# A block with a selective scan, attention and routed experts on one core: scores computed twice, probabilities never turned

## The reference, cut to what matters

```python
x = x + tanh(g_xattn) * ssm_forward(ctx_1024, layernorm(x), ...)
# in the second part, per batch element:
q, k = rope(h @ wq + bq, h @ wk + bk);  v = h @ wv + bv
scores = einsum('bqhd,bkhd->bhqk', q, k) * HEAD_DIM ** -0.5
scores = where(causal, scores, finfo.min)
attn = softmax(scores, axis=-1)
ctx = einsum('bhqk,bkhd->bqhd', attn, v);  x = x + ctx @ wo
# scan, per step t:
state = state * exp(d_t * A) + (d_t * u_t) * B_t;  y_t = state . C_t
```

## Time and profile before

| | |
|---|---|
| median of 3 runs | 1940.85 us (1940.26 to 1944.68) |
| profiled execution, its own time | 1938.13 us |
| its span, first to last instruction | 1936.3 us |
| busy: PE, PEld | 1546.4 us (80%), 1184.4 us (61%) |
| busy: DVE, ACT, POOL | 1221.5 us (63%), 888.3 us (46%), 786.2 us (41%) |
| mean granted clock of TensorE, of full | 0.853 |

### The profile page before, as it was taken

One profiled execution on the slowest core, in us unless ns is written; L12 is line 12 of the kernel. 1 busy time (PEld: TensorE's weight loads), 2 busy tenths in 40 slices (PEclk: granted clock), 3 DMA queues, 4 the chain that ended last, 5 costly groups with the idle time before them and its releaser, 6 DMA issues.

```text
span 1936.3 us, 26458 instructions
## 1 busy us (share of the span) xinstructions
PE 1546.4 (80%) x9104; PEld 1184.4 (61%) x9104; DVE 1221.5 (63%) x1730; ACT 888.3 (46%) x1973; POOL 786.2 (41%) x744
## 2 busy tenths in 40 slices
PE   5346877777957778767769676899999999999994
PEld 2234544455635555544547444778878899999973
DVE  4789669987488986599873452433232566656545
ACT  3433446664356662566642564121121466666510
POOL 0595145542255441355432021144321455555544
PEclk8555977888967788968889687999999999999997
DMA  5620001110101110001101111812120477777464
GB/s 192 235 77 22 23 11 33 55 45 27 40 22 50 53 36 28 11 28 55 45 23 66 55 34 50 347 63 101 60 71 1 183 251 263 244 252 258 156 234 157
DMA packets 92372, 191.54 MB, mean 99 GB/s; under 512 B 8704, under 2 KB 25600, under 8 KB 88912
## 3 DMA queue, kind: packets, MB, share of 16 engines
q1 hardware_dynamic: 87120, 173.07, 26.0%
q0 software_dynamic: 5120, 16.78, 2.6%
HBM read 136.21 MB, written 53.61 MB: 98 GB/s over the span
## 4 chain that ended last, share of the span: by engine, by line
PE 40%; DVE 6%; issue 5%; ACT 3%; POOL 3%; DMA 0%; DVEq 0%; ACTq 0%; SPq 0%; POOLq 0%
PE scores L526 21%; PE bank L526 12%; DVE HS L1370 2%; POOL yab L1924 2%; PE scores L645 1%; DVE YA L1380 1%; PE bank L673 1%; PE bank L658 1%; PE bank L823 1%; PE bank L590 1%; ACT EX L1035 1%; ACT PT L1043 1%; ACT bank L1000 1%; DVE nm L1422 1%; POOL lal L1917 1%
## 5 line engine op out<-in xcount | busy, mean ns | idle before, releaser
L1781 POOL TENSOR_TENSOR GB<-DU,BB 128x512 f32<-128x512 f32 x256 | 327.4, 1292 | 138.8 <-DVE HS L1370 83.4
L590 PE MATMUL bank<-ident,HS 128*128 128x128 f32 x896 | 190.8, 351 | 181.0 <-DVE YA L1380 126.4
L1370 DVE TENSOR_TENSOR_SCAN HS<-bank,GB 128x512 f32<-128x512 f32 x224 | 270.4, 1207 | 33.7 <-ACT bank L1000 15.5
L590 PEld LDWEIGHTS bank<-ident,HS 128*128 128x128 f32 x896 | 128.7, 176 | 231.8 <-DVE YA L1380 167.2
L1000 ACT ACTIVATE bank<-DL,aneg 128x512 f32<-128x512 f32 x224 | 155.0, 692 | 139.3 <-DVE HS L1370 138.0
L1380 DVE SCALAR_TENSOR_TENSOR YA<-bank,Ct,YA 128x512 f32<-128x512 f32 x224 | 164.8, 736 | 27.5 <-PE bank L590 25.2
L526 PE MATMUL scores<-xth,wgh 128*128 128x256 f32 x552 | 158.0, 286 | 2.0 <-DVE fa L1667 1.1
L1043 ACT ACTIVATE PT<-bank 128x128 f32<-128x128 f32 (+3 forms) x256 | 110.3, 431 | 107.2 <-PE bank L658 106.2
L526 PE MATMUL scores<-xth,wgl 128*128 128x256 f32 x552 | 156.1, 283 | 0.0
L526 PE MATMUL scores<-xtl,wgh 128*128 128x256 f32 x552 | 156.0, 283 | 0.0
L658 PE MATMUL bank<-ident,EX 128*128 128x128 f32 x640 | 132.5, 316 | 26.5 <-ACT PT L1043 24.9
(11 more groups left out here) (241 smaller groups left out, 3816.4 us busy)
## 6 DMA issues: line engine op xcount, KB each, us to landing
wgr<-wffn_in SPq DMA_DIRECT2D x108, 384.0 KB, 6.5
wdr<-wffn_in SPq DMA_DIRECT2D x81, 256.0 KB, 3.2
BB<-b_scratch SPq DMA_DIRECT2D x64, 256.0 KB, 3.2
xg<-V SPq DMA_DIRECT2D x1, 11776.0 KB, 39.2
xr<-xg SPq DMA_DIRECT2D x23, 512.0 KB, 5.7
yg<-ysb SPq DMA_DIRECT2D x23, 512.0 KB, 6.4
hah<-hhd SPq DMA_DIRECT2D x5, 1024.0 KB, 6.0
hal<-hhd SPq DMA_DIRECT2D x5, 1024.0 KB, 8.0
```

Source lines behind the costliest of these rows:

```text
L590: mm = nc.tensor.transpose(state_bank(s, q)[:, et * P:(et + 1) * P], HS[:, n % 2, et, tt * P:(tt + 1) * P], ident[:])
L1370: nc.vector.tensor_tensor_scan(HS[:, n % 2, et, :], decay_bank(s, k), GB[:, k % 4, :], 0.0, ALU.mult, ALU.add).then_inc(scan_done, 1)
L1781: nc.gpsimd.tensor_tensor(GB[:, k % 4, :], DU[:, et, :], BB[:, n % 2, :], ALU.mult).then_inc(gb_ready, 1)
```

## The change

The scores of a quad are computed twice. The first time they serve the maxima alone. Those are written to column 0 of each head's 32 in `nm` (128 x 4 x 32, zero elsewhere), transposed by TensorE (`turn_max`), and copied to `nmT` by ScalarE (`keep_max`). `turned_scores` then seeds `SB` with the maxima (a row of ones, `first`, times `nmT`, over all key blocks), and adds the products of keys and queries with the keys as rows of the result, and the turned mask. One exponential over all four heads gives probabilities that already stand turned, in `EX`, which now has two buffers. `weigh` takes them as the stationary operand and V as the moving one; V has a 33rd column of ones per head, which gives the sums. VectorE takes the reciprocal of the 128x4 sums and scales; the context is then transposed (`turn_context`) and copied twice by ScalarE. It runs one quad later than before.

The decays use two banks (`HT1`, `PB`) in all rounds. `finish` moves within the quads of a block. Two loads share a semaphore, and a few memsets are added at the start.

```diff
-        def decay_bank(s, k):
-            return (HT1, A[1])[k % 2] if s == 0 else HT1
+        def decay_bank(k):
+            return (HT1, PB)[k % 2]
...
+            def turn_max(b, q):
+                pe.wait_ge(mx_done, NQ * b + q + 1)
+                nc.tensor.transpose(A[0][:, 0:P], nm[:].rearrange("p a d -> p (a d)"), ident[:]
+                                    ).then_inc(mt_mm, 1)
+
+            def turned_scores(b, q):
...
+                pe.wait_ge(mt_done, NQ * b + q + 1)
+                for a in range(HG):
+                    r = HD * a
+                    nc.tensor.matmul(SB[:, a, 0:W], first[r:r + HD, :],
+                                     nmT[r:r + HD, :].unsqueeze(1).broadcast_to([HD, i + 1, P]), start=True, stop=False)
                 for kb in range(i + 1):
+                    for a in range(HG):
+                        r = HD * a
+                        nc.tensor.matmul(SB[:, a, kb * P:(kb + 1) * P], QK[r:r + HD, 4 + m, kb * P:(kb + 1) * P],
+                                         QK[r:r + HD, m, i * P:(i + 1) * P], start=False, stop=False)
+                for a in range(HG):
+                    mm = nc.tensor.matmul(SB[:, a, W - P:W], maskb[:], identb[:], start=False, stop=True)
+                mm.then_inc(st_mm, 1)
 
             def weigh(b, q):
...
+                pe.wait_ge(ex_done, NQ * b + q + 1)
+                at(pe, cc_done, NQ * b + q)
+                at(pe, cth_done, NQ * b + q)
+                for a in range(HG):
+                    for kb in range(i + 1):
+                        mm = nc.tensor.matmul(CX[:, a * (HD + 1):(a + 1) * (HD + 1)],
+                                              EX[:, q % 2, a, kb * P:(kb + 1) * P], V[:, kb, HG * m + a, :],
+                                              start=(kb == 0), stop=(kb == i))
                 mm.then_inc(pv_mm, 1)
...
+            def probs(b, q):
                 W = P * (quad(q)[0] + 1)
+                act.wait_ge(st_mm, NQ * b + q + 1)
+                at(act, pv_mm, NQ * b + q - 1)
+                nc.scalar.activation(EX[:, q % 2, :, 0:W], SB[:, :, 0:W], ACT.Exp).then_inc(ex_done, 1)
...
             def context(b, q):
+                dve.wait_ge(pv_mm, NQ * b + q + 1)
+                whole = CX[:, 0:HG * (HD + 1)].rearrange("p (a d) -> p a d", d=HD + 1)
+                nc.vector.reciprocal(ri[:], whole[:, :, HD]).then_inc(ri_done, 1)
+                dve.wait_ge(ri_done, NQ * b + q + 1)
                 at(dve, ctl_done, NQ * b + q)
+                nc.vector.tensor_tensor(cn[:].rearrange("p (a d) -> p a d", d=HD), whole[:, :, 0:HD],
+                                        ri[:].unsqueeze(2).broadcast_to([P, HG, HD]), ALU.mult).then_inc(cn_done, 1)
```

More of the change, by code:

```diff
@@ L740, in round_ @@
                     i, m = quad(q)
+                    if att:
+                        turn_max(b, q)
+                    if scn and q:
+                        turn_states(s, T4 * (q - 1))
+                    if att and q >= 2:
+                        turn_context(b, q - 2)
+                    if att:
+                        turned_scores(b, q)
+                    if scn and q:
+                        turn_states(s, T4 * (q - 1) + 1)
+                    if att and q:
+                        weigh(b, q - 1)
+                    if scn and q:
+                        turn_states(s, T4 * (q - 1) + 2)
                     if att and q + 1 < NQ:
                         scores(b, q + 1)
-                    for a in range(HG):
-                        if att:
-                            turn(b, HG * q + a)
-                        if scn and q:
-                            turn_states(s, T4 * (q - 1) + a)
-                        if att and i and (m, a) in ((0, 1), (2, 1), (3, 2)):
-                            finish(b, i - 1, (0, 0, 1, 2)[m])
-                    if att:
-                        weigh(b, q)
+                    if att and i and m:
+                        finish(b, i - 1, m - 1)
+                    if scn and q:
+                        turn_states(s, T4 * (q - 1) + 3)
+                if att:
+                    turn_context(b, NQ - 2)
+                    weigh(b, NQ - 1)
+                    turn_context(b, NQ - 1)
                 if scn:
@@ L1501, in round_ @@
                     k = T4 * q
-                    more = att and q + 1 < NQ
                     if scn:
                         scan(s, k)
-                    if att and q:
-                        context(b, q - 1)
-                    if more:
-                        row_max(b, q + 1)
                     if scn and q:
@@ L1516, in round_ @@
                         scan(s, k + 2)
+                    if att and q:
+                        context(b, q - 1)
                     if scn and q:
                         add_state(s, k - 2)
-                    if att and i and m != 1:
-                        finish(b, i - 1, (1, 0, 2, 3)[m])
                     if scn:
                         scan(s, k + 3)
+                    if att and q + 1 < NQ:
+                        row_max(b, q + 1)
                     if scn and q:
                         add_state(s, k - 1)
-                    if more:
-                        invert(b, q + 1)
+                    if att and i and m:
+                        finish(b, i - 1, m)
                     if s == B and q == 11:
@@ L1852, in round_ @@
                     k = T4 * q + 2
-                    if att and i and m == 1:
-                        finish(b, i - 1, 0)
-                    if att and i and m == 3:
-                        finish(b, i - 1, 1)
-                    for a in range(2):
-                        if scn and k + a < NB:
-                            driven(s, k + a)
-                    if att and q:
-                        context(b, q - 1)
+                    if scn and k < NB:
+                        driven(s, k)
+                    if att and q >= 2:
+                        context(b, q - 2)
+                    if scn and k + 1 < NB:
+                        driven(s, k + 1)
+                    if att and i and m >= 2:
+                        finish(b, i - 1, m - 2)
                     for a in range(2, 4):
@@ L1969, in _ @@
             pool.wait_ge(rows_made, 5)
-            nc.gpsimd.memset(V[:, 0, :], 0.0).then_inc(zt_made, 1)
+            nc.gpsimd.memset(V[:, 0], 0.0).then_inc(rows_made, 1)
+            nc.gpsimd.memset(first[:], 0.0).then_inc(rows_made, 1)
+            nc.gpsimd.memset(nm[:], 0.0).then_inc(rows_made, 1)
+            pool.wait_ge(rows_made, 8)
+            for a in range(HG):
+                nc.gpsimd.memset(first[HD * a:HD * a + 1, :], 1.0).then_inc(rows_made, 1)
             for r in range(-1, B):
```

169 lines of the change are left out of this document (63 added, 106 removed).

## The result

| us | before | after |
|---|---|---|
| median of 4 runs each | 1942.76 (1940.26 to 1945.50) | 2037.87 (2026.08 to 2047.87) |
| ratio, 95% interval | | 1.049, 1.045 to 1.052 |
| profiled execution / span | 1938.1 / 1936.3 | 2047.9 / 2046.1 |
| TensorE busy | 1546 (80%) | 1715 (84%) |

A forecast was written before the change was run, and what follows sets the result against it. VectorE was taken to bound mixed rounds, in blocks 0 and 1 and nearly in 2 and 3. Three mixed rounds at +5 us (+15) and attention alone +13 gave +28, a median of 1969 us; range 1920 to 2004.

The forecast's parts named there:

- So 0.77 us goes per quad, 12.3 us in a mixed round.: VectorE in mixed rounds: the reciprocal shrinks from 128x128 to 128x4, saving 0.77 us a quad, 12.3 us a round.
- blocks 2 and 1: 2.35 and 1.7: Turned scores, seed to mask, priced at full clock: 2.35 us in block 2, 1.7 in block 1, 3.0 in block 3.
- the exponential 1.98, weigh "2.7" in block 2: Per quad: ScalarE's exponential of 2048 columns takes 1.98 us; TensorE's weigh in its new form takes 2.7 in block 2.
- decay(k+2) queued behind the exponential: ScalarE, mixed rounds: decay(k+2) waits behind the exponential, so scans wait some 2 us per quad in blocks 2 and 3.
- The second bank idle since its decays queue behind the exponential: Mixed rounds: the second decay bank brings nothing; said within the case of about 1941 us, chance 0.17.
- the rival of cancelling: Rival: tighter packing in the mixed rounds pays for the loss in attention alone, about 1941 us; chance 0.17.
- With a tenth of the 140 us at half clock, +4 to +5. I take +5 a round.: Mixed rounds: +1 us at full clock in blocks 1 to 3, a tenth at half clock; +5 a round, +15 for three.
- 2.5 for the last, longer weigh: End of a mixed round: the last weigh, in its longer new form, adds 2.5 us to the round's sum.
- less 1 at the end: Attention alone: 1 us taken off at the end of the stretch, in its sum of 134 us against 122 before.
- +12, and +1 for half clock: Attention alone: no scan covers the new chain, 134 us against 122, +12, plus 1 for half clock, +13 in all.
- The clock falls: Rival: TensorE idles during row_max, a third of blocks 1 to 3 at half clock; +70, 2011 us; chance 0.15.
- VectorE decides: Rival, faster: turned_scores packs tighter and clock stays full; -8 us a mixed round, 1923 as a median; chance 0.22.

The follow-up runs named there:

- b1_decay_first: Kernel after, with the quad's second decay put before the exponential on ScalarE instead of behind it: 2021.68 us, 1.040 of the kernel before.
- a1_one_bank: Kernel after, with a single decay bank (HT1) in every round, each decay waiting for the scan before it: 2065.94 us, 1.063 of the kernel before.
- c3_mixed_filler: Kernel after, with unused filler products on TensorE in attention quads, mixed rounds too, and one decay bank in mixed rounds: 2025.14 us, 1.040.
- b3_wide_sums: Kernel after, with V and repeated ones stationary in weigh, probabilities moving, no context turn, reciprocal 128x128 again: 2003.00 us, 1.030 of the kernel before.
- a2_thin_weigh: Kernel after, with weigh reduced to the last key block, four products a quad: 2003.72 us, 1.030 of the kernel before.
- finish and tail alone: Two edits of the kernel after: finish behind the quad's last turn of states, 2034.68 us; a round's last states before its last weigh, 2038.29 us.
- The fillers: Kernel after with unused TensorE products: in attention alone 2029.69 us; in mixed rounds too, with one decay bank there, 2025.14 us.
- b4_all: Kernel after, with V and ones stationary in weigh, second decay before exponential, finish behind last state turn, last states before last weigh: 1969.06 us, 1.015.

## Why the prediction was wrong

The sign and the list of what is added held, and of the signs that it named only the scans' wait was not found. The loss was 3.4 times the forecast. Two steps failed; the other points show what held and what was right by luck.

- **"So 0.77 us goes per quad, 12.3 us in a mixed round."** Right: 12.4.
- **"blocks 2 and 1: 2.35 and 1.7", the exponential 1.98, weigh "2.7" in block 2.** The last two are right: 1.88 and 2.76 (24 records) were measured. The turned scores were priced too high at full clock. With 0.25 on top until the exponential starts the sum had 3.25, 2.6 and 1.95 us in blocks 3, 2 and 1. At full clock the mask has ended after 2.36, 1.92 and 1.49, and the exponential starts 0.04 later (442.67 us). That is some 8 us a round too much, which by luck hid as much of what the clock took.
- **"decay(k+2) queued behind the exponential"**, some 2 us per quad of waiting scans in blocks 2 and 3. The queue is real (`b1_decay_first`), the named wait was not found: scans wait 8.2 us a round for decays, 5.4 before. A late scan may meet a TensorE that has meanwhile gone on to longer work, so that the time shows as add_state's wait for turned states; no run shows this.
- **"The second bank idle since its decays queue behind the exponential"**, said within the rival of cancelling: no run speaks against it for the mixed rounds (`a1_one_bank`), though the sum that went with it was wrong.
- **"With a tenth of the 140 us at half clock, +4 to +5. I take +5 a round."** This is the first step that failed. The chain that is new was priced at full clock, from the earlier trace rows, and set against blocks of before as measured, at theirs. The earlier trace rows showed 0.83, 0.82 and 0.95 for blocks 1 to 3, which is a quarter of their time at 1.2 GHz, not a tenth. The step's own price, 0.35 us lost per us at half clock, times a quarter of 140 gives +12 a round, +13 with the 1 at full clock. Blocks 1 to 3 rose by 14.2, 9.7 and 7.7 us in the three rounds. But a mean of the block is the wrong figure as well: the chain's own products run right behind the gap that the change makes, at 0.50 to 0.63 in nine quads of twelve of round 0. Behind it stands a sum that I did not make: TensorE's busy time beside the block's. Products that I counted only as links of a chain brought it from 128 of 177 us to 150 of 180, and the states' turns queue in it.
- **"2.5 for the last, longer weigh"** and in attention alone **"less 1 at the end"**. The second step that failed. The tails cost 10.5, 6.2, 8.1 and 11.8 us, 36.6 instead of 6.5. The weigh that ends them runs at half clock (7.01 us, a bound that the prediction had and did not take here), and it waits for the context of the quad before to be out of its bank, which was in no term: the exponential ended at 1281.5, weigh began at 1288.4.
- **Attention alone, "+12, and +1 for half clock".** Block by block the forecast was +5.9, -1.2, +4.0, +4.4; measured +6.8, +5.5, +10.2, +5.6. Block 0, priced at half clock, and block 3 fit. Blocks 1 and 2 were priced at full clock and got 0.76 and 0.74. Block 3 was priced so too and got 0.79, so that it fits is in part luck.
- **The rivals.** "The clock falls" (2011, chance 0.15) was nearest, for a reason that it had only partly: the mean clock of the mixed blocks did not fall, but more work came to depend on it, and at its low moments. Its price, with a third at half clock, was +48 for the mixed rounds and +25 alone, 73 in all. The trace's 66 and 40 exceed that by 33, and the tails beyond their forecast are 30. "VectorE decides" is out: VectorE was 158 of round 0's 217 us busy. Of its two conditions the tighter packing came true and the full clock did not. Where a run had both, in round 0 of `c3_mixed_filler`, blocks 1 to 3 took 123.6 us, and that rival's figures for them (three quads of block 3) add up to 123.7. It is one round, with a single decay bank.

What is shown: weigh in its new form, with the turn and copies behind it, is the largest single cost that an edit took back (`b3_wide_sums` -35, `a2_thin_weigh` -34), the order of decay and exponential the next (-16), and finish and tail alone are below what the runs tell. The trace shows besides that the added products ran at half clock behind their own gap, 42 us over their time at full clock in blocks 1 to 3 of four rounds, and in one round of `c3_mixed_filler` the blocks gained as much as these products did. What stays open is how the mixed rounds' loss splits between the chain and the clock. The fillers changed TensorE's load as well, in two of the three rounds of `c3_mixed_filler` they did not pay, no run sets the clock alone, and why the same instructions get another clock in another execution or program is not known. Of the 28 us that `b4_all` still loses, the wait for turned states is named, not undone.

## To carry to other kernels

Put the busy time of every engine after the change, stretch by stretch and at the clock that this stretch's rows show, beside the chain's length: one that goes from 72% to 83% busy can delay everyone who queues on it. When rows for a new chain are at full clock and the old one is taken as measured, price the new one at the old one's clock first, and look for an idle stretch of TensorE right ahead of it: the products behind one may have half clock even where the block's mean is 0.87. Look at a stretch that an edit does not touch before you read one that it does. Small operands belong on the side that is loaded: at full clock 32 records with 128 columns loaded and 33 moving took 3.66 us, twice as many with 32 loaded and 128 moving 1.96.

## What was not expected of the hardware

- The same instructions of attention alone, block 2, took 48.8, 42.2 and (with some 60 filler records) 36.8 us at granted clocks of 0.61, 0.74 and 0.92. Edits elsewhere in the program moved which it was. The kernel after spread over 22 us in four runs, the kernel before over 5 in its first four and over 18 in 13 later ones.
- Leaving out key-query products gained nothing (2040.66 against 2037.87): the mean clock of an execution fell from 0.834 to 0.851 (four runs) to 0.816 to 0.819.
- Products that compute nothing made the kernel before 0.4% faster (interval 0.1 to 0.7%), and did nothing for `b4_all`.
